# Two graph layers over 8 graphs: rows of x gathered with their place in the sorted order, in place of a second reading of the adjacency matrix and scattered tables

## The reference

```python
# layer 0: at most the first 25 neighbours, maximum over their rows
scores = where(adj != 0, -arange(N), -inf);  vals, idx = top_k(scores, 25)
agg = max over valid neighbours of x[idx];   agg = max(agg, 0) where degree <= 25
x1 = layernorm(x + relu(concat(x, agg) @ W0 + b0))
# layer 1: attention of 8 heads of 32 over the neighbours
Wh = x1 @ W1;  s1, s2 = Wh . a1, Wh . a2            # one number per node and head
e = leaky(s1[i] + s2[j] + edge_emb[adj]);           # masked where adj == 0
h = softmax(e) @ Wh;  out = layernorm(x1 + elu(layernorm(h) * gamma + beta))
```

## Time and profile before

| | |
|---|---|
| three runs | 3204.43 us median (3190.37 to 3209.11) |
| the profiled execution | 3204.28 us, span of its instructions 3202.6 us |
| DVE | 2501.0 us busy, 78% |
| POOL | 2280.8 us busy, 71% |
| PE | 2098.0 us busy, 66% |
| ACT | 1218.3 us busy, 38% |
| transfers | 644.16 MB, mean 201 GB/s; 208 loads of adjacency tiles |
| granted TensorE clock | 0.799 of full speed in the mean |

### The profile page before, as it was taken

One profiled execution on the slowest core, in us unless ns is written; L12 is line 12 of the kernel. 1 busy time (PEld: TensorE's weight loads), 2 busy tenths in 40 slices (PEclk: granted clock), 3 DMA queues, 4 the chain that ended last, 5 costly groups with the idle time before them and its releaser, 6 DMA issues.

```text
span 3202.6 us, 30987 instructions
## 1 busy us (share of the span) xinstructions
PE 2098.0 (66%) x7199; PEld 1505.5 (47%) x7203; DVE 2501.0 (78%) x5719; ACT 1218.3 (38%) x2779; POOL 2280.8 (71%) x2376
## 2 busy tenths in 40 slices
PE   7446566865566666767677777766676756568565
PEld 2224334643344444555455555544454544356454
DVE  5697677888787887788888898889886776567776
ACT  3223334443344334434444444423332322224334
POOL 3276476677777777777777777777777777777774
PEclk9767676877677788887878878888888967779887
DMA  6676667766666667777777777766655545445443
GB/s 231 213 240 230 220 227 252 236 224 202 206 226 220 221 212 238 237 229 238 243 230 251 241 233 243 218 187 201 189 160 143 161 125 141 126 132 165 125 129 100
DMA packets 271980, 644.16 MB, mean 201 GB/s; under 512 B 67505, under 2 KB 170930, under 8 KB 245170
## 3 DMA queue, kind: packets, MB, share of 16 engines
q0 software_dynamic: 111360, 309.05, 32.7%
q1 hardware_dynamic: 160434, 333.08, 30.4%
HBM read 572.07 MB, written 69.86 MB: 200 GB/s over the span
## 4 chain that ended last, share of the span: by engine, by line
POOL 39%; DVE 20%; issue 17%; PE 13%; DMA 4%; DVEq 4%; ACT 3%; SPq 0%; POOLq 0%; ACTq 0%
POOL ring L728 37%; DVEq L1169 4%; PE score_p L985 4%; DVE pay L1217 3%; DVE agg L1398 3%; PE lin_p L1020 3%; PE att_p L1057 2%; DVE ring L1537 2%; DVE agg L1388 1%; DMA sorted_d<-srt 1%; DVE pick L1277 1%; DVE adj_h L1204 1%; ACT adj_i L797 1%; PE wh_p L1036 1%; PE lin_p L1018 1%
## 5 line engine op out<-in xcount | busy, mean ns | idle before, releaser
L728 POOL DMA_INDIRECT ring<-table_d,idx x1096 | 1055.0, 963 | 364.1 <-issue 331.1
L1057 PE MATMUL att_p<-ring,ident 128*128 128x256 f32 (+1 forms) x2384 | 655.3, 438 | 311.4 <-ACT x_t L835 227.8
L728 POOL DMA_INDIRECT ring<-sorted_d,idx x685 | 677.1, 989 | 208.7 <-issue 206.0
L1057 PEld LDWEIGHTS att_p<-ring,ident 128*128 128x128 f32 (+1 forms) x2384 | 518.8, 222 | 449.3 <-issue 286.0
L728 POOL DMA_INDIRECT ring<-in_x_dram,idx x411 | 396.5, 965 | 257.4 <-DVEq L1343 125.2
L1398 DVE TENSOR_REDUCE agg<-ring 128x256 f32<-128x2560 f32 (+9 forms) x120 | 455.5, 3796 | 69.4 <-DMA ring<-sorted_d,idx 51.2
L1020 PE MATMUL lin_p<-w_s,h_t 128*128 128x256 f32 x1024 | 412.5, 573 | 0.0
L985 PE MATMUL score_p<-pay,pick 128*128 128x322 f32 x1024 | 344.7, 485 | 27.5 <-DVE pick L1277 19.1
L1020 PEld LDWEIGHTS lin_p<-w_s,h_t 128*128 128x128 f32 x1024 | 278.6, 285 | 115.4 <-issue 61.2
L866 ACT ACTIVATE neg<-z 128x256 f32<-128x256 f32 x128 | 53.4, 417 | 725.5 <-DVE z L1440 725.4
L1537 DVE TENSOR_TENSOR ring<-ring,score_p 128x1536 f32<-128x1536 f32 (+10 forms) x128 | 320.7, 2505 | 9.8 <-issue 0.3
(11 more groups left out here) (200 smaller groups left out, 3357.1 us busy)
## 6 DMA issues: line engine op xcount, KB each, us to landing
adj_i<-in_adj_dram SPq DMA_DIRECT2D x208, 1024.0 KB, 5.8
sorted_d<-srt SPq DMA_DIRECT2D x128, 161.0 KB, 6.4
ring<-table_d,idx POOLq DMA_INDIRECT x1096, 2.9
pay<-in_x_dram SPq DMA_DIRECT2D x32, 512.0 KB
xs<-sorted_d SPq DMA_DIRECT2D x128, 128.0 KB
fin_d<-res SPq DMA_DIRECT2D x112, 128.0 KB, 5.8
fin<-fin_d SPq DMA_DIRECT2D x28, 512.0 KB, 6.8
out_dram<-turned_out SPq DMA_DIRECT2D x112, 128.0 KB
```

The source lines that it names most:

```text
L728: pool.indirect_dma_start(out=to[:, k * width:(k + 1) * width], out_offset=None, in_=source, in_offset=bass.IndirectOffsetOnAxis(ap=idx_at ...
L1057: last = pe.matmul(att_p[:, 0:C], ident[0:on, :], r3[0:on, s, 0:C], start=(s == 0), stop=(s == k - 1))
```

## The change

All graphs are now handled alike. The column code is the column's own number throughout. When a group is ranked, `rank_rows` writes each node's place into column 256 of its row in `pay`, and SP stores the 257 columns of the group in the old order to a new table `nat_d` (`store_places`, 32 times). Layer 0 gathers from `nat_d` by the old numbers and gets 257 columns a row. Ahead of its maximum, `index_places` casts the places that came with the rows into the index tile, over the numbers just used; these are layer 1's indices. So its table is stored by SP in sorted order for all graphs, and the pass of degrees, the turned codes, the scatters and `index_local` are gone.

```diff
-OWN = C + CAND
+PLACE = C
+XROW = C + 1
+OWN = XROW + CAND
...
             def load_pay(g):
                 if g >= 2:
                     sp.wait_ge(permuted, PERM_AT["in", GROUP * (g - 1) - 1] + 1)
+                    sp.wait_ge(nat_st[g % 2], 16 * (g // 2))
...
+            def store_places(g):
+                b, at = g // GROUP, g % GROUP * GN
+                sp.wait_ge(pay_ld[g % 2], 16 * (g // 2 + 1))
+                sp.wait_ge(place_put, g + 1)
+                sp.dma_start(nat_d[b][at:at + GN, :].rearrange("(t p) c -> p t c", p=P),
+                             pay3[:, GROUP * (g % 2):GROUP * (g % 2 + 1), 0:XROW]).then_inc(nat_st[g % 2], 16)
...
             for r in range(ROUNDS):
                 n = r + AHEAD
+                if ranked_in(r - 1) is not None:
+                    store_places(ranked_in(r - 1))
...
-                if first(r - 6) and (r - 6) // T >= RANKED:
+                if first(r - 6):
                     store_table(r - 6)
...
-                for k in CASTS_OF[r]:
-                    if k + 2 < len(CASTS):
-                        load_adj(k + 2)
+                if n + 4 < TILES:
+                    load_adj(n + 4)
...
-                source = table_d[b] if layer else x_rows if b < RANKED else sorted_d[b]
+                source = table_d[b] if layer else nat_d[b]
...
+                    if u == 0:
+                        for q in range(2):
+                            pool.wait_ge(nat_st[q], 16 * (GROUP // 2) * (b + 1))
                 elif i % T == 0:
-                    if 1 <= b < RANKED:
-                        pool.wait_ge(idx_local, b)
+                    pool.wait_ge(idx_local, b + 1)
                     for q in range(4):
-                        if b < RANKED:
-                            pool.wait_ge(tab_out[q], 16 * (T // 4) * (b + 1))
-                        else:
-                            pool.wait_ge(tab_st[q], 16 * (T // 4) * (b + 1 - RANKED))
+                        pool.wait_ge(tab_st[q], 16 * (T // 4) * (b + 1))
...
-                for i in tables_in(r):
-                    scatter_table(i)
...
-                if kind == "degree":
-                    act.activation(adj_i[q][:, :].bitcast(F32), adj_i[q][:, :], ACT.Copy,
-                                   accum_out=degree[:, n:n + 1]).then_inc(cast_done, 1)
-                    return
...
+                need(dve, nat_st[g % 2], 16 * (g // 2))
+                v.tensor_scalar(pay3[:, GROUP * (g % 2):GROUP * (g % 2 + 1), PLACE], mine, float(GROUP),
+                                float(g % GROUP), ALU.mult, ALU.add).then_inc(place_put, 1)
...
+            def index_places(i, rows):
+
+                b, u = tile0(i)
+                q, pair = b % 3, pair_of(0, i)
+                places = rows.rearrange("p (k c) -> p c k", c=XROW)[:, PLACE, :]
+                n = FULL if u == 0 else SLOTS[u] - 1 if pair else SLOTS[u]
+                last = v.tensor_copy(idx_part(b, u // PART)[:, u % PART, 0:n], places[:, 0:n])
+                if u == 0:
+                    v.tensor_copy(top[q][:, :], places[:, FULL:FULL + 2])
+                if pair and not pair[2]:
+                    v.tensor_copy(pair_i[q][:, pair[0]:pair[0] + 1], pair_s[0][:, PLACE:PLACE + 1])
+                if u == T - 1:
+                    last.then_inc(idx_local, 1)
...
                 rows = ring_tile(0, i)
+                c3 = rows.rearrange("p (k c) -> p c k", c=XROW)
+                index_places(i, rows)
...
-                    last = v.tensor_reduce(a, rows.rearrange("p (k c) -> p c k", c=C), AX, ALU.max)
+                    last = v.tensor_reduce(a, c3[:, 0:C, :], AX, ALU.max)
```

More of the change, by code:

```diff
@@ L77 @@
 CONSTS0 = 7
-CONSTS = 51
+CONSTS = 50
 ORDER1 = [6, 14, 11, 0, 2, 4, 13, 15, 1, 3, 5, 8, 10, 7, 9, 12]
@@ L92, in tile1 @@
     return b, (w if b == B - 1 else ORDER1[w])
[L95 to L115, removed]
-def ranked_in(r):
[L120 to L136, removed]
+def ranked_in(r):
+    n = r + AHEAD
+    return n // GROUP if 0 <= n < TILES and n % GROUP == GROUP - 1 else None
 def in_step(k):
@@ L240, in build @@
         sorted_d = [nc.dram_tensor(f"sorted_d{b}", (N, SENT), F32).ap() for b in range(B)]
+        nat_d = [nc.dram_tensor(f"nat_d{b}", (N, XROW), F32).ap() for b in range(B)]
         table_d = [nc.dram_tensor(f"table_d{b}", (N, ROW), F32).ap() for b in range(B)]
@@ L265, in build @@
         turned_out = [sb(f"turned_out{q}", [P, C]) for q in range(2)]
-        idx_raw = sb("idx_raw", [P, PART * (SENT - C)])
-        idx = [sb(f"idx{q}", [P, PART * (sum(LISTED) + 2)], I32) for q in range(3)]
+        idx_raw = sb("idx_raw", [P, PART * (SENT - XROW)])
+        idx = [sb(f"idx{q}", [P, PART * sum(LISTED)], I32) for q in range(3)]
         top = [sb(f"top{q}", [P, 2], I32) for q in range(3)]
@@ L383, in build @@
         rank_used = sem("rank_used")
-        code_put = sem("code_put")
-        code_ready = sem("code_ready")
+        place_put = sem("place_put")
+        nat_st = [sem(f"nat_st{q}") for q in range(2)]
         pay_ld = [sem(f"pay_ld{q}") for q in range(2)]
@@ L473, in ring_tile @@
             u = (tile1(i) if layer else tile0(i))[1]
-            width = ROW if layer else C
+            width = ROW if layer else XROW
             at = RING_AT[layer, i] * ROW
@@ L593, in _ @@
                 load_adj(n + 3)
+                if n % GROUP == 0 and n:
+                    store_places(n // GROUP - 1)
                 for x in PERMS_OF_STEP[n]:
@@ L892, in _ @@
                     elu(j - 3)
-                for k in CASTS_OF[r]:
-                    if CASTS[k][0] == "search":
-                        cast(k)
+                if first(r + AHEAD + 2):
+                    cast(r + AHEAD + 2)
                 if first(r - 5):
@@ L910, in _ @@
                     copy_perm(perms[1])
-                for k in CASTS_OF[r]:
-                    if CASTS[k][0] == "degree":
-                        cast(k)
             def body(b):
@@ L992, in permute @@
                 last.then_inc(permuted, 1)
-            def codes(b):
-                pe.wait_ge(code_put, b - RANKED + 1)
-                pe.wait_ge(cast_used, (b - 1) * T)
-                for c in range(T):
-                    last = pe.transpose(code_p[:, P * c:P * (c + 1)],
-                                        code_h[:, c:c + 1].broadcast_to([P, P]), ident_h[:, :])
-                last.then_inc(code_ready, 1)
             def turn(i):
@@ L1080, in _ @@
                     attend(j - 1)
-                b = coded_in(r - 2)
-                if b is not None:
-                    codes(b)
                 if first(r - 3):
```

107 lines of the change are left out of this document (28 added, 79 removed).

## The result

The changed kernel took 3125.47 us (3121.50 to 3126.23, 4 runs) against 3203.11 us (3190.37 to 3209.11) for the kernel before: a ratio of 0.976, 95% interval 0.973 to 0.979. The forecast was 3131 us. The profiled span fell from 3202.6 to 3123.9 us. Beside the experiments one execution of the kernel before took 4263 us, and the ratios there leave it out.

The account below looks back on a forecast made before the run. POOL's rate of gathers was taken as the bound behind 637 us, the rounds of DVE, PE and ACT before. Savings of 51 + 33 - 11 = 73 us gave a span of 3129.6 and 3131 us; range 3085 to 3175 us.

Parts of the forecast that it names:

- 51 - 3 - 2 = 46 us: Before 637 us: 51 us saved by dropping the degree pass and rankings, less 3 for casts and 2 for stores of places.
- 84 us cover the 51: Before 637 us: POOL's 58 us of standing and 26 us of scatters were said to let it use the 51 us saved.
- the additions: Added casts, small copies and stores of places: 11 us of cost in all, ends 3 and 40 us.
- 33 - 6 = 27 us: Behind 637 us: 33 us saved on scatters and waits for tables, less 6 us for added DVE casts and copies.
- I take three quarters: Behind 637 us: of 44 us from scatters and table waits, 33 us counted by the chain's 75%, since DVE can't always follow.
- its one row (2.25 us): A gather starting just before two picks takes 2.25 us; cited as a rule speaking against the added casts.
- The signs: Trace marks named beforehand, such as gathers at 0.95 + 0.30 us if right, a 2304-element maximum away from 4.1 us if wrong.
- POOL stays full: Rival: POOL full from the second graph on, all its savings count; 100 us off, 3104 us; chance 18%.
- DVE takes over: Rival: behind 637 us only 10 of 33 us are left and small operations count whole; 36 us off, 3168 us; chance 13%.
- the casts lock POOL: Rival: the added casts and copies lock POOL out, 30 us more than forecast, 3161 us; chance 6%.
- my sentence that the trace agrees for the picks: Claim that the trace's picks, but not a 64x256 copy, fit the skill's rule that two-port DVE operations lock GpSimd out.
- Slower: Rival: layer 0's maximum costs more at 1028-byte steps; gain gone from 2.2 ns an element, about 3260 us at 2.6; chance 6%.

## Why the prediction was right

**Before 637 us.** Forecast 51 - 3 - 2 = 46 us; measured 46.1 at that gather. The total is right, its parts were not. I put the loads and casts of degrees at 40 us, the rankings at 7 + 4 us and the scatters at nothing, "84 us cover the 51". In the run with both parts back the loads and casts cost 20.9 us on top of the scatters, about half of the 40; alone they cost 44.7. The scatters cost 12.5 us alone, where the sum had nothing, and -11 us on top of the degrees. So the step that failed is the one that priced each part by itself: what a part costs ahead of 637 us depends on which others are there. 12.7 us of the 46.1 are left that neither part nor both put back. The rankings by degree, less the additions, are a candidate, but no run isolates them, and by the medians both parts together put back everything (3206 for 3203 us). That such errors cancel to within 1 us is luck. The wait for the second graph's indices ends 15.5 us sooner (364.0 to 348.5 us), not 20.

**Behind 637 us.** Forecast 33 - 6 = 27 us; measured 77.7 - 46.1 = 31.6 us, as 42.7 gained up to gather 800 and 11.1 lost again. The mis-sized step is "I take three quarters": POOL could use all 44 us, since DVE followed (43.0 us for the scatters alone up to gather 800). I had expected POOL to wait 10 us more for ring slots; those waits are 2.7 + 1.5 us now. The 11 us lost are the term that the sum didn't have, and that it offsets the step before is luck once more. They are longer gathers: between gathers 800 and 1700 the surplus grew by 12.2 us. Behind gather 323 it grew by 9.7 us, 6.9 of them beside picks. The prediction saw the effect at its one row (2.25 us) but looked for it in the new casts, and not in the old picks. Fewer gathers lie beside picks (195 for 208), but 85 instead of 59 start in the picks' first 0.9 us, where they are long, and 17 instead of 50 at their end, where they take 1.0 us. What set the gathers against the picks in this way stays open. It isn't the loss of scatters and degree casts: with both put back the time is that of the kernel before, but the surplus behind gather 323 is still 60.2 us. I tried nothing that moves gathers against picks.

**The additions.** Casts at 9 us (3 + 6): 7.0 in one pair of traces, 4.6 of them ahead of gather 323 (forecast 3) and 2.4 behind (forecast 6), and 2 us by the medians; neither is clear of chance. The first gather starts at 136.5 instead of 133.9 us (forecast 2 us later). With the same stores and loads of places ahead of it the later runs have it between 135.3 and 138.9 us, so the 2.6 us are known only roughly. A gather of 1028 bytes costs POOL what one of 1024 did: 988 ns in the mean for `nat_d`, and 989 before for `sorted_d`, both with what the picks add.

**The signs.** The waits for roots fell to 2.3 us (forecast near 6), and gathers still take 0.95 + 0.30 us. Two signs of being wrong showed too: the maximum of 2304 elements takes 4254 ns, and POOL waits 11.2 us for tables before 509 us, now that SP stores them. Neither was in the sum. POOL's waits for ring slots are 4.2 us and did not grow by 10.

**The rivals.** "POOL stays full" had the right mechanism behind 637 us and the wrong size ahead of it. "DVE takes over" fell with DVE's share of the chain (9%, before 20%), "the casts lock POOL" with the run without casts. The Trainium skill ("SBUF — State Buffer", "Who interferes with whom") names copies, casts and operations of a tensor with a scalar as those that can enter a mode in which they lock GpSimd out, and says that a DVE operation with two inputs in SBUF contends with a GpSimd operation that reads SBUF. This case agrees on the second, if a gather counts as such an operation (its offsets lie in SBUF): gathers were held by such picks, 1.37 us in the mean of 85 for 0.95 us. The same section infers that an operation of two tensors leaves the issue of a DMA from GpSimd alone; here it doesn't, and the measurement decides. Of the first this case shows little: without the casts the gathers' surplus was the same, those that started in the first 0.9 us of picks with scalars kept 0.98 us in the mean, and 13 that started with a copy of 32x528 had 1.00 us, the longest 1.18. So my sentence that the trace agrees for the picks took the wrong rule: that section gives an operation of two tensors no mode of two ports, and the picks belong under its rule on two inputs. "Slower" was partly true: the maximum of 2304 elements takes 4254 instead of 4091 ns (4%), that of 3328 elements 6172 instead of 5791 ns (7%). It stayed far from the 2.2 ns an element: by the prediction's own difference it is (4254 - 2339) / 1024 = 1.87 ns for 1.71. POOL's 4.2 us of waits for ring slots leave next to nothing of it on the path behind 591 us.

## What to carry to other kernels

A gain worked out part by part depends on the order in which the parts go: here each was worth some 28 us first and 52 us last, so put parts back both alone and together before you call a size known. Where POOL's own issue of gathers is the bound, look at which DVE operations overlap its longest ones; a comparison against a scalar instead of a second tensor brought 22 us and cost only DVE time that was free. Don't read the price of a part off one wait: a cast of a tenth the length left SP waiting as long as before, and yet brought 28 us.

## What the runs showed of the hardware

- A DVE operation with two tensors in SBUF delays an indirect gather that starts with it (2.00 us beside 1.27 us of picks, 2.43 us beside 1.68; 1.14 us beside 0.48 us of L1357), though not each one: the shortest beside a pick kept 0.94 us. The same comparison with a scalar per partition left 0.98 us in the mean of 84, and operations with their second input in PSUM 0.947 us, however long (L1415, L1454).
- A maximum along an outer axis depends on the step between rows: 16 rows took 7104 ns at 1024 bytes, 7475 at 1028 and 7505 at 1056; 9 rows 4091, 4254 and 4296; 5 rows 2341, 2339 and 2428. Why 1024 bytes is the cheapest isn't settled; the casts ahead of the maximum aren't the reason, since the kernel without them has 4253 ns for 9 rows.
- One chip ran the kernel before in 4088 instead of 3201 us. In the run with the degrees a gather took 966 ns there as elsewhere, and ACT stood 605 us before a buffer that a store must leave. A part sized on one chip has another size there: on top of the scatters the degrees cost 90 us, and 28 us on the others.
